# Cross attention with a mixture-of-experts stage: bias columns, norm seeds, tanh and first units' splits at other ticks, mask rows at once

## Chip, cores, metric

One Trainium2 chip, one core. The metric is the device time of the whole kernel in microseconds. Three runs of the kernel before gave 1059.28, 1064.75 and 1064.88 us, median 1064.75.

## What is computed

Eight batches of 512 tokens, 256 wide, with a context of 512 tokens, 512 wide, all in float32:

```python
x = x + xattn(ctx, layernorm(x), mask, mask, W_src, b_src, W_tgt, b_tgt, W_out, b_out)
x = x + ffn(layernorm(x), ...)
# xattn: k, v = split((ctx @ W_src.T + b_src) * mask); q = (x @ W_tgt.T + b_tgt) * mask
#        8 heads of 32; softmax(q k / sqrt(32)) with masked keys at -inf; times v
#        cat(x, update) @ W_out.T + b_out
# ffn:   scores = sigmoid(l2norm(x) @ l2norm(gate).T), top 8 of 16 experts, weights / their sum
#        sum over experts of w * (silu(x @ wg) * (x @ wu)) @ wd, and a shared expert beside them
```

## The kernel before, in words

Every engine runs the same ordered list of steps, and each takes from it what concerns it, in order. Between engines there are only semaphore waits; an instruction that waits holds up all that is behind it on its engine. A matrix product in near-float32 precision is made of three: each operand is split into a high part (a rounding copy, mostly on ScalarE) and a low part (a subtraction on VectorE or GpSimd), and TensorE does hi*hi, hi*lo and lo*hi.

**The attention stage.** `attention()` gives each step a tick, a number on a common scale, and sorts the steps by tick (equal ticks in the order in which they were listed). Work is in 16 groups (g), two per batch, of four heads each. A group takes 16 ticks: each tick holds one matmul for the row maxima (`max`, L732, in PSUM banks 0 and 1, reduced by VectorE at L1201 14 ticks ahead of the group) and one scores matmul (`scores`, L748), whose result goes through the exponential on ScalarE (L868, the helper of all ScalarE copies) into one of seven `e_buf` slots. GpSimd adds four of these (`e_add`, L1407) for the softmax sums, and `attend` multiplies them with v (L759) and ones (L772). The projections of later groups, q, k, v and y, lie between at ticks of their own, in three PSUM banks used in turn. `hi_q`, `hi_k`, `lo_k` split q and k, and `stack` copies the splits by DMA from the SP queue (ScalarE's queue has a part of the first two) into `q_stack` and `k_stack`; row 96 of `k_stack` is the mask bias (`bias_row`), row 97 of `q_stack` the negated maxima (`shift`, `neg`). The high part of the next group's q may be written only when the stacks of the group before have landed.

**The start.** The first steps stand in a list `first` at tick -42.4. The bias of v goes through the output weights: VectorE spreads it to 128 columns (L1182, the tile shares space with `e_buf`), TensorE multiplies (L790), VectorE adds to the bias rows (L1185), and GpSimd adds these to x (`x_bo`). All of that is the step `bo` at tick -13.8, behind the operations of the second batch's layer norm (`ln1`, ticks from -26.2).

**The mask.** For each batch c the mask row comes broadcast to 128 partitions; `mask_bias` on VectorE (L1155) turns one row of 512 elements into 0 or -1e30, at 2.7 ticks after the beginning of each pair of groups, in one of two row buffers.

**The way into the second stage.** For batch 0, `ln2` (33 steps on VectorE, GpSimd and ScalarE; steps 8 and 9 compute `ve` on GpSimd, L1359 and L1361, steps 10 and 11 are VectorE's seeds for the inverse root, L1070 and L1072, then GpSimd goes on) lies in group 13; `gating` (16 steps on VectorE, of which the third multiplies the logits by the norm, L1267, and the fourth needs ScalarE's tanh) in group 14. Six units of experts (`gate_up` 0 to 5) are laid in group 15 and behind it. For a unit, TensorE computes gate and up into two banks; ScalarE the silu (for the first four units as a tanh), VectorE the products (L1301, L1304, L1309), ScalarE the high part hh, VectorE the low part; `down` multiplies by the third weight matrix. All of ScalarE's and VectorE's part of a unit stands at the tick of its `gate_up`. `early_w` splits weights on ScalarE and GpSimd; `turn_c` turns the combine weights, and `load_c` spreads them by DMA over 128 partitions.

**The second stage.** The other 130 units follow in a fixed order, each `gate_up` with the `down` of two units before.

## Time and profile before

| | us |
|---|---|
| median of three runs | 1064.75 |
| lowest, highest | 1059.28, 1064.88 |
| span of the profiled execution | 1056.2 |
| TensorE busy | 1012.5 (96%) |
| VectorE busy | 647.5 (61%) |
| ScalarE busy | 465.9 (44%) |
| GpSimd busy | 389.0 (37%) |

The span is that of the first to the last instruction of one execution; no other time is given for it. Shares are averages over the whole span: GpSimd, VectorE and ScalarE do most of their work in the first 480 us. A matmul counts as busy until its modelled end, at either clock.

### The profile page before, as it was taken

The numbers are of one execution on the slowest core, as the hardware profiler recorded it, in microseconds if no ns is written. First come the engines' busy times: TensorE is split into PE (matmuls) and PEld (weight loads), VectorE is DVE, ScalarE is ACT, GpSimd is POOL, SyncE is SP. The second block draws the span as 40 slices with busy tenths as digits, with TensorE's granted clock in tenths as the row PEclk, the third lists the DMA queues.
The fourth block names the chain that finished last, engine by engine and source line by source line (L and its number), as shares of the span: only waits on it lengthen the run. The fifth ranks groups of instructions, "written<-read, shape, count | busy, mean of one in ns | idle before, by whom it ended". The sixth has DMA issues, their size and how long they took to land.

```text
span 1056.2 us, 14941 instructions
## 1 busy us (share of the span) xinstructions
PE 1012.5 (96%) x5198; PEld 773.3 (73%) x5198; DVE 647.5 (61%) x1469; ACT 465.9 (44%) x865; POOL 389.0 (37%) x355
## 2 busy tenths in 40 slices
PE   4789999999999998899999999999999999999998
PEld 3656767676767665567888888888888888888886
DVE  5877777877777557355565555555555555555544
ACT  3346565656665646545323323333333333332322
POOL 3379797879797967345210010010010100100000
PEclk9899999999999999999999999999999999999999
DMA  7343433434333223324222121121220230221220
GB/s 239 104 131 78 131 81 111 108 84 131 73 110 75 65 65 105 92 86 131 75 80 61 52 80 50 61 81 40 72 80 31 71 90 20 91 80 31 93 68 20
DMA packets 65674, 87.87 MB, mean 83 GB/s; under 512 B 10720, under 2 KB 31088, under 8 KB 65600
## 3 DMA queue, kind: packets, MB, share of 16 engines
q1 hardware_dynamic: 63680, 84.83, 28.0%
q10 hardware_dynamic: 1920, 2.10, 0.6%
q8 instruction: 41, 0.67, 0.3%
q14 instruction: 33, 0.27, 0.1%
HBM read 56.97 MB, written 4.46 MB: 58 GB/s over the span
## 4 chain that ended last, share of the span: by engine, by line
PE 91%; DVE 4%; ACT 2%; SPq 1%; issue 1%; DMA 1%; POOL 0%; DVEq 0%; ACTq 0%
PE ps L653 50%; PE pst L653 18%; PE ps L732 6%; PE ps L759 5%; PE pst L748 5%; PE ps L659 4%; PE ps L772 1%; DVE mx L1201 1%; ACT e_buf L868 1%; SPq L606 1%; PE ps L811 1%; SPq L541 1%; ACT ctx_h L868 0%; DVE wsrc_l L1148 0%; PE ps L812 0%
## 5 line engine op out<-in xcount | busy, mean ns | idle before, releaser
L653 PE MATMUL ps<-x_h,weights 128*128 128x512 f32 x1088 | 365.6, 397 | 1.4 <-DVE x L1194 0.8
L653 PEld LDWEIGHTS ps<-x_h,weights 128*128 128x128 f32 x1088 | 204.5, 188 | 51.8 <-issue 1.0
L1201 DVE TENSOR_REDUCE mx<-ps 128x1 f32<-128x512 f32 x256 | 173.3, 685 | 81.8 <-PE ps L732 80.9
L868 ACT ACTIVATE hh<-qb 128x512 fp32r<-128x512 f32 x136 | 86.0, 632 | 296.4 <-DVE qb L1315 273.7
L653 PE MATMUL ps<-x_l,weights 128*128 128x512 f32 x544 | 214.6, 395 | 0.0
L653 PE MATMUL pst<-hh,weights 128*128 128x512 f32 x544 | 194.6, 399 | 0.0
L1304 DVE TENSOR_TENSOR qb<-ps,sg 128x512 f32<-128x512 f32 x136 | 94.1, 692 | 160.2 <-PE ps L653 153.8
L868 ACT ACTIVATE e_buf<-pst 128x512 f32<-128x512 f32 x256 | 147.4, 596 | 92.8 <-PE pst L748 81.8
L1317 DVE TENSOR_TENSOR hl<-qb,hh 128x512 fp32r<-128x512 f32 x136 | 94.3, 693 | 95.0 <-ACT hh L868 95.0
L1407 POOL TENSOR_TENSOR e_sums<-e_sums,e_buf 128x1024 f32<-128x1024 f32 x60 | 143.5, 2391 | 7.2 <-ACT e_buf L868 1.2
L1359 POOL TENSOR_SCALAR ve<-mv 128x4 f32<-128x4 f32 x8 | 1.8, 226 | 347.1 <-DVE mv L1242 347.1
L653 PEld LDWEIGHTS ps<-x_l,weights 128*128 128x128 f32 x544 | 102.1, 188 | 24.6
L748 PE MATMUL pst<-q_stack,k_stack 98*128 98x512 f32 x256 | 108.4, 425 | 12.1 <-ACT e_buf L868 12.0
L868 ACT ACTIVATE sg<-ps 128x512 f32<-128x512 f32 x136 | 81.1, 596 | 86.6 <-PE ps L653 86.6
L653 PEld LDWEIGHTS pst<-hh,weights 128*128 128x128 f32 x544 | 102.2, 188 | 23.3 <-DVE hl L1317 0.8
L732 PE MATMUL ps<-k_stack,q_stack 97*128 97x512 f32 x256 | 109.7, 430 | 6.7 <-DVE mx L1201 6.2
L653 PE MATMUL pst<-hl,weights 128*128 128x512 f32 x272 | 107.3, 394 | 0.0
L1315 DVE TENSOR_TENSOR qb<-qb,cb 128x512 f32<-128x512 f32 x124 | 87.4, 705 | 4.2
L1407 POOL TENSOR_TENSOR e_sums<-e_buf 128x1024 f32<-128x1024 f32 x30 | 71.8, 2394 | 48.8 <-PE ps L772 48.3
L732 PEld LDWEIGHTS ps<-k_stack,q_stack 97*128 97x128 f32 x256 | 49.2, 193 | 46.0 <-issue 29.1
L748 PEld LDWEIGHTS pst<-q_stack,k_stack 98*128 98x128 f32 x256 | 49.4, 194 | 27.1 <-ACT e_buf L868 16.6
L759 PE MATMUL ps<-e_buf,v_buf 128*32 128x512 f32 x512 | 62.1, 603 | 0.0
(159 smaller groups left out, 1391.5 us busy)
## 6 DMA issues: line engine op xcount, KB each, us to landing
cb<-combine_scratch SPq DMA_DIRECT2D x128, 256.0 KB, 3.2
q_stack<-q_h SPq DMA_DIRECT2D x128, 64.0 KB, 2.0
k_stack<-k_h SPq DMA_DIRECT2D x124, 64.0 KB, 2.0
ctx_raw<-in_ctxT SPq DMA_DIRECT2D x7, 1024.0 KB, 5.2
q_stack<-q_l SPq DMA_DIRECT2D x64, 64.0 KB, 2.0
out_x<-ob SPq DMA_DIRECT2D x16, 256.0 KB, 2.2
k_stack<-k_l SPq DMA_DIRECT2D x62, 64.0 KB, 2.0
x<-in_x SPq DMA_DIRECT2D x7, 512.0 KB, 6.5
```

The source lines that it names most:

```text
L541: e.dma_start(f32(KS[g % 2][at:at + 32, h, :]), f32(src[32 * h:32 * h + 32, :])).then_inc(sem(f"stack{g % 2}{h}"), 16)
L653: ins = engine.matmul(dst, lhsT, rhs, start=start and n == 0, stop=stop and n == len(terms) - 1)
L659: ins = engine.transpose(dst, src, ID[0:k, 0:k])
L732: engine.matmul(ps, QS[z][0:97, h, 128 * q:128 * q + 128], KS[z][0:97, h, :], start=True, stop=True).then_inc(sem("s_max"), 1)
L748: engine.matmul(YP[:, m % 2, :], KS[z][0:98, h, 128 * k:128 * k + 128], QS[z][0:98, h, :], start=True, stop=True).then_inc(sem("s_t"), 1)
L759: ins = engine.matmul(OP[32 * i:32 * i + 32, :], VB[:, b % 2, k, hh + i, :], EB[:, SLOTS[8 * g + 4 * (i // 2) + k], i % 2, :], start=k == ...
L868: return engine.activation(dst, src, func, **kw)
L1201: engine.tensor_reduce(MX[:, g % 2, h // 2, h % 2, q:q + 1], bank(step), AX.X, ALU.max).then_inc(sem("max"), 1)
L1304: engine.tensor_tensor(QB[:, w, :], GP[n][1], SG[:, w, :], ALU.mult).then_inc(sem("hq"), 1)
L1315: engine.tensor_tensor(QB[:, w, :], QB[:, w, :], CB[:, m % NC, :], ALU.mult).then_inc(sem("hc"), 1)
L1317: engine.tensor_tensor(HLB[:, n % NH, :], QB[:, w, :], f32(HHB[:, n % NH, :]), ALU.subtract).then_inc(sem("h_lo"), 1)
L1407: engine.tensor_tensor(ES[:, a, :, :], first, EB[:, SLOTS[n + 1 + i], :, :], ALU.add).then_inc(sem("e_add"), 1)
```

## The change

The steps that change place or kind:

- `mask_bias`: one step in `first`. A new DMA on SP, ahead of the small bias loads, brings all eight mask rows into partitions 32 to 39 of `shift_rows`, and one VectorE operation of 8 x 512 converts them. `bias_row` reads the row of its batch. The seven later operations, and the waits for them on SP and GpSimd, go; `shift_rows` is half as long per partition.
- `bo`: VectorE's two column copies become the step `bv`, in `first` ahead of v; the TensorE part `bo` follows v and `out_q` there; the addition `bo_add` stays at -13.8. q of the second group moves ahead of both halves of v.
- the splits and first stack of the third group (p = 2): 2.6 ticks later.
- `ln2` of batch 0: the first ten steps from 2.6 in steps of 0.3 (before 3.1 in steps of 0.4), the others from 8 in steps of 0.33 (before they began at 7.1).
- `gating` of batch 0: three steps as before, the others from 6.8 in steps of 0.35 (before from 5.5 in steps of 0.4); the tanh goes with the fourth (6.8) and no more with the first (4.3). `turn_c` and four `load_c` from 12.7 to 14.8.
- the units: `silu`, `unit`, `hi_h`, `lo_h` are steps of their own; for the first six they are 0.5, 0.6, 2.4 and 2.5 ticks behind their `gate_up`. In the second stage they directly follow it, in the same order as before.

```diff
-        if half == 0:
-            at(t + 2.7, ("mask_bias", c))
-        at(t + 5.4, ("hi_q", p))
-        at(t + 6.4, ("hi_k", p))
-        at(t + 7.1, ("lo_k", p))
-        at(t + 7.1, ("stack", p, 0))
+        late = 2.6 if p == 2 else 0
+        at(t + 5.4 + late, ("hi_q", p))
+        at(t + 6.4 + late, ("hi_k", p))
+        at(t + 7.1 + late, ("lo_k", p))
+        at(t + 7.1 + late, ("stack", p, 0))
...
-             ("load_ctx", 1), ("k", 0, 0), ("k", 0, 1), ("mask_bias", 0), ("ws_hi", 1), ...
+             ("load_ctx", 1), ("k", 0, 0), ("k", 0, 1), ("mask_bias",), ("ws_hi", 1), ...
-             ("v", 0, 0, 0), ("q", 1), ("v", 0, 0, 1), ("out_q", 1), ("out_v", 0, 0), ("bias_row", 1)]
+             ("q", 1), ("bv",), ("v", 0, 0, 0), ("v", 0, 0, 1), ("out_q", 1), ("bo",), ("out_v", 0, 0), ("bias_row", 1)]
...
-    at(-13.8, ("bo",))
+    at(-13.8, ("bo_add",))
...
-        at(t + 3.1 + 0.4 * i, s)
+        at(t + (2.6 + 0.3 * i if i < 10 else 8 + 0.33 * (i - 10)), s)
...
-        at(t + 4.3 + 0.4 * i, s)
-    at(t + 12.7, ("turn_c", 0), *[("load_c", m) for m in range(NC)])
+        at(t + (4.3 + 0.4 * i if i < N_TANH else 6.8 + 0.35 * (i - N_TANH)), s)
+    at(t + 14.8, ("turn_c", 0), *[("load_c", m) for m in range(NC)])
...
+    for n, when in enumerate((3.6, 7.2, 13, 16.2, 25.3, 26.6)):
+        at(t + when + 0.5, ("silu", n))
+        at(t + when + 0.6, ("unit", n))
+        at(t + when + 2.4, ("hi_h", n))
+        at(t + when + 2.5, ("lo_h", n))
...
-        shift_rows = s1("shift_rows", [97, 2, S], F32R)
-        MR, NM, OR = shift_rows[96:97, :, :], shift_rows[0:8, 0, 0:128], shift_rows[64:65, 0, :]
+        shift_rows = s1("shift_rows", [65, S], F32R)
+        MR, NM, OR = shift_rows[32:32 + B, :], shift_rows[0:8, 0:128], shift_rows[64:65, :]
...
+                    engine.dma_start(f32(MR), mask).then_inc(sem("ld_rows"), 16)
...
-                    dve.wait_ge(*mask_loaded(b))
-                    if b > 1:
-                        dve.wait_ge(*row_loaded(2 * b - 3))
-                    engine.tensor_scalar(MR[:, b % 2, :], MB[96:97, b % 2, :], 0.0, MASKED, ALU.is_equal,
-                                         ALU.mult).then_inc(sem("mask_bias"), 1)
+                    dve.wait_ge(sem("ld_rows"), 16)
+                    engine.tensor_scalar(MR[:, :], f32(MR[:, :]), 0.0, MASKED, ALU.is_equal, ALU.mult).then_inc(
+                        sem("mask_bias"), 1)
```

## Rows read from the trace of the kernel before

**Rows 1.** The page's picture in 40 slices: TensorE's busy tenths.

```profile
PE   4789999999999998899999999999999999999998
```

**Rows 2.** The list of waits on TensorE: total us, times, longest us.

```profile
PE pst L748 <- ACT e_buf L868: 12.0, 12, 2.5
```

**Rows 3.** Table by stretches; after the engines' busy us: granted clock, DMA share, GB/s.

```profile
core 0: us, PE busy (x) PEld busy (x) DVE busy (x) ACT busy (x) POOL busy (x), PEclk, DMA share, GB/s
31.40:35.30 3.90, 3.87 (x15) 3.51 (x16) 2.05 (x9) 0.00 (x0) 1.57 (x1) 0.56 0.42 103
35.30:44.90 9.60, 9.05 (x55) 7.53 (x54) 7.50 (x20) 3.88 (x8) 3.74 (x3) 1.00 0.36 112
48.70:56.10 7.40, 7.05 (x19) 4.52 (x17) 4.84 (x11) 4.53 (x10) 5.25 (x5) 0.54 0.44 106
390.00:395.00 5.00, 5.00 (x30) 2.48 (x29) 2.23 (x4) 1.37 (x3) 3.36 (x6) 0.66 0.35 85
415.00:420.00 5.00, 5.00 (x28) 2.88 (x27) 4.97 (x20) 4.00 (x9) 4.95 (x4) 0.75 0.26 79
```

**Rows 4.** Timeline of the start, SP and TensorE: start us, us, what, idle before.

```profile
2.71 0.88 SPq L533 DMA_DIRECT2D mask_rows<-in_mask  x1
...
21.81 0.39 PE L653 MATMUL ps<-wsrc_h,ctx_h 128*128 128x256 f32 x1 [1.21 <-DVE wsrc_l L1148]
...
31.43 1.68 PE L790 MATMUL ps<-e_buf 128*128 128x256 f32 x4 [3.44 <-DVE e_buf L1182]
```

**Rows 5.** Timeline of the start, VectorE.

```profile
21.68 0.74 DVE L1175 SCALAR_TENSOR_TENSOR k_l<-ps,bk,k_h 128x512 fp32r<-128x512 f32 x1
24.93 0.75 DVE L1170 SCALAR_TENSOR_TENSOR f_buf<-ps,bt,mask_rows 128x512 f32<-128x512 f32 x1 [2.51 <-PE ps L653]
...
30.86 0.47 DVE L1182 TENSOR_SCALAR e_buf<-ones_sb,bv 128x128 f32<-128x128 f32 x2
33.15 0.42 DVE L1185 TENSOR_TENSOR bo_rows<-ps,bo_rows 128x256 f32<-128x256 f32 x1 [1.82 <-PE ps L790]
```

**Rows 6.** Timeline 55 to 60 us, GpSimd, VectorE, TensorE.

```profile
55.80 2.38 POOL L1407 TENSOR_TENSOR e_sums<-e_buf 128x1024 f32<-128x1024 f32 x1
...
56.30 2.17 DVE L1155 TENSOR_SCALAR shift_rows<-mask_rows 1x512 fp32r<-1x512 f32 x1
...
59.25 0.50 PE L732 MATMUL ps<-k_stack,q_stack 97*128 97x512 f32 x1 [0.97 <-DVE mx L1201]
```

**Rows 7.** All mask operations: duration ns min/median/max, first and last start us.

```profile
L1155 DVE TENSOR_SCALAR shift_rows<-mask_rows x8: 424/1556/2171, 18.6 to 353.3; 1x512 fp32r<-1x512 f32 x8
```

**Rows 8.** Timeline 62 to 64 us, ScalarE and TensorE.

```profile
62.77 0.63 ACT L868 ACTIVATE q_h<-f_buf 128x512 fp32r<-128x512 f32 x1 [5.23 <-DMA k_stack<-k_l]
...
63.93 0.50 PE L748 MATMUL pst<-q_stack,k_stack 98*128 98x512 f32 x1 [1.35 <-ACT e_buf L868]
```

**Rows 9.** Timeline 388 to 390 us, VectorE and TensorE.

```profile
388.17 0.17 DVE L1070 TENSOR_SCALAR rs_a<-ve 128x8 int32<-128x8 int32 x1 [2.82 <-POOL ve L1361]
...
389.29 0.47 PE L732 MATMUL ps<-k_stack,q_stack 97*128 97x512 f32 x1 [2.29 <-DVE mx L1201]
```

**Rows 10.** Timeline 410 to 414 us, GpSimd, VectorE, TensorE.

```profile
410.55 2.35 POOL L1407 TENSOR_TENSOR e_sums<-e_sums,e_buf 128x1024 f32<-128x1024 f32 x1
...
411.18 1.80 DVE L1267 TENSOR_TENSOR lg<-lg,rn 128x64 f32<-128x64 f32 x1
...
413.90 0.59 PE L748 MATMUL pst<-q_stack,k_stack 98*128 98x512 f32 x1 [2.46 <-ACT e_buf L868]
```

**Rows 11.** Timeline 434 to 452 us, ScalarE and TensorE.

```profile
434.19 0.60 ACT L868 ACTIVATE sum_sb<-ps 128x512 f32<-128x512 f32 x1
...
441.38 0.63 ACT L868 ACTIVATE hh<-qb 128x512 fp32r<-128x512 f32 x1 [2.82 <-DVE qb L1309]
...
442.55 0.98 PE L748 MATMUL pst<-q_stack,k_stack 98*128 98x512 f32 x2 [2.47 <-ACT e_buf L868]
...
451.45 0.47 PE L653 MATMUL ps<-x_h,weights 128*128 128x512 f32 x1 [0.64 <-DVE sg L1301]
```

**Rows 12.** The page's costliest groups, one product of a unit on VectorE.

```profile
L1304 DVE TENSOR_TENSOR qb<-ps,sg 128x512 f32<-128x512 f32 x136 | 94.1, 692 | 160.2 <-PE ps L653 153.8
```

More of the change, by code:

```diff
@@ L47 @@
 N_LN1, N_LN2, N_GROWS, N_GATE = N_SMALL1 + 4, N_SMALL2 + 4, 3 + rsqrt_steps(1) + 3, 16
+N_TANH = 3
 TODO = [(b, e) for b in range(B) for e in range(E + 1)]
@@ L121, in attention @@
              ("ctx", 0, 3), ("ws_hi", 0), ("q", 0), ("ws_lo", 0), ("out_q", 0), ("hi_q", 0),
-             ("load_ctx", 1), ("k", 0, 0), ("k", 0, 1), ("mask_bias", 0), ("ws_hi", 1), ("hi_k", 0), ("ws_lo", 1), ("lo_k", 0),
+             ("load_ctx", 1), ("k", 0, 0), ("k", 0, 1), ("mask_bias",), ("ws_hi", 1), ("hi_k", 0), ("ws_lo", 1), ("lo_k", 0),
              ("bias_row", 0), ("stack", 0, 0), ("stack", 0, 1), ("stack", 0, 2), ("stack", 0, 3), ("wo",),
-             ("v", 0, 0, 0), ("q", 1), ("v", 0, 0, 1), ("out_q", 1), ("out_v", 0, 0), ("bias_row", 1)]
+             ("q", 1), ("bv",), ("v", 0, 0, 0), ("v", 0, 0, 1), ("out_q", 1), ("bo",), ("out_v", 0, 0), ("bias_row", 1)]
     at(-42.4, *first)
@@ L259, in order @@
             load_c(b * E + min(e, E) + NC)
-            out.append(("gate_up", n))
+            out += [("gate_up", n), ("silu", n), ("unit", n), ("hi_h", n), ("lo_h", n)]
             if b + 1 < B:
@@ L583, in sync_program @@
                     sp.wait_ge(sem("q_f"), 2 * b - 2)
-                    sp.wait_ge(sem("mask_bias"), b - 1)
                     load_mask(engine, b)
@@ L591, in sync_program @@
                     g = step[1]
-                    sp.wait_ge(sem("mask_bias"), g // 2 + 1)
+                    sp.wait_ge(sem("mask_bias"), 1)
                     if g > 1:
                         sp.wait_ge(*scores_done(g - 2, 3))
-                    row = MR[:, (g // 2) % 2, :].rearrange("a (h s) -> a h s", h=1).to_broadcast([1, 4, S])
+                    row = MR[g // 2:g // 2 + 1, :].rearrange("a (h s) -> a h s", h=1).to_broadcast([1, 4, S])
                     engine.dma_start(f32(KS[g % 2][96:97, :, :]), f32(row)).then_inc(sem(f"bias_row{g % 2}"), 16)
@@ L616, in sync_program @@
                     sp.wait_ge(sem("x_bo"), B)
-                    sp.wait_ge(sem("mask_bias"), B)
                     for e in range(NR):
@@ L1020, in scalar_program @@
                     copy(X2h[:, b % 2, j, :], bank(step)).then_inc(sem("x2_hi"), 1)
-                elif kind == "gating" and step[2] == 0:
+                elif kind == "gating" and step[2] == N_TANH:
                     b = step[1]
@@ L1035, in scalar_program @@
                     act.wait_ge(sem("ut_lo"), NG)
-                elif kind == "gate_up":
+                elif kind == "silu":
                     n = step[1]
@@ L1048, in scalar_program @@
                         copy(SG[:, n % 2, :], GP[n][0], ACT.Silu).then_inc(sem("silu"), 1)
+                elif kind == "hi_h":
+                    n = step[1]
                     b, e = TODO[n]
@@ L1150, in vector_program @@
                 elif kind == "mask_bias":
-                    b = step[1]
-                    dve.wait_ge(*mask_loaded(b))
-                    if b > 1:
-                        dve.wait_ge(*row_loaded(2 * b - 3))
-                    engine.tensor_scalar(MR[:, b % 2, :], MB[96:97, b % 2, :], 0.0, MASKED, ALU.is_equal,
-                                         ALU.mult).then_inc(sem("mask_bias"), 1)
+                    dve.wait_ge(sem("ld_rows"), 16)
+                    engine.tensor_scalar(MR[:, :], f32(MR[:, :]), 0.0, MASKED, ALU.is_equal, ALU.mult).then_inc(
+                        sem("mask_bias"), 1)
                 elif kind == "lo_x":
@@ L1177, in vector_program @@
                                                     sem("k_lo"), 1)
-                elif kind == "bo":
+                elif kind == "bv":
                     for k in range(2):
@@ L1183, in vector_program @@
                             sem("bv_cols"), 1)
+                elif kind == "bo_add":
                     dve.wait_ge(sem("bo_t"), 1)
-                    engine.tensor_tensor(BO[:, :], bank(step)[:, 0:D], BO[:, :], ALU.add).then_inc(sem("bo"), 1)
+                    engine.tensor_tensor(BO[:, :], bank(("bo",))[:, 0:D], BO[:, :], ALU.add).then_inc(sem("bo"), 1)
                 elif kind == "out_y":
@@ L1291, in vector_program @@
                     dve.wait_ge(sem("y"), COUNT["y", B - 1, 1, 1])
-                elif kind == "gate_up":
+                elif kind == "unit":
                     n = step[1]
@@ L1315, in vector_program @@
                         engine.tensor_tensor(QB[:, w, :], QB[:, w, :], CB[:, m % NC, :], ALU.mult).then_inc(sem("hc"), 1)
+                elif kind == "lo_h":
+                    n = step[1]
+                    w = n % 2
                     dve.wait_ge(sem("h_hi"), n + 1)
@@ L1422, in gpsimd_program @@
                     pool.wait_ge(sem("y_add"), COUNT["out_y", B - 1, 0, 1])
-                    pool.wait_ge(sem("mask_bias"), B)
                 elif kind in ("early_w", "split_w"):
```

## The prediction, made before the result was known

> **What bounds the kernel now.** I read the picture in slices first: TensorE is busy nine tenths or more in every slice from the fourth on but two, and from about 475 us to the end it has no gap worth a row [rows 1]. So the second half is TensorE's own work, which the edits leave alone, and a gain must come from the holes before 475 us. Second, the list of waits: the largest item is the scores matmul waiting for an exponential on ScalarE (12.0 us in 12 places) [rows 2]. Third, the table by stretches, for the clock: behind three of the holes, and once more near 50 us, the granted clock is a mix of 1.2 and 2.4 GHz [rows 3]. A clock of 0.56 over 3.9 us loses 0.44 x 3.9 = 1.7 us of work; 0.54 over 7.4 us loses 3.4; 0.66 over 5 us loses 1.7; 0.75 over 5 us loses 1.25. Last, the timelines around each hole, to see which instruction was in front of the one TensorE needed.
>
> The sum is made against the profiled span, 1056.2 us. The three runs lie 3.1 to 8.7 us above it (median 1064.75), and the page has no other time of that execution, so the difference found here is taken off the median.
>
> **Start, 20 to 45 us.** Before, TensorE waits 1.21 us for the second half of the source weights, and later 3.44 us for the two bias-column copies [rows 4], which stand on VectorE behind 34 small norm operations although their input landed long ago; the copies take 0.47 us [rows 5]. After it, the clock is low for 1.7 us worth of work [rows 3]. The change puts q of the second group into the first hole (six matmuls fill it) and the copies ahead of the norm chain. TensorE alone would gain 1.21 + 3.44 + 1.7 = 6.35 us. VectorE allows less: its f_buf operation starts at 24.93 after 2.51 us of waiting [rows 5]; with q early it follows k_l (21.68 + 0.74) and the copies (0.47) [rows 5], at about 22.9, so 2.0 us earlier. It then no longer runs the copies in the chain (0.47) nor waits for the bo matmul (1.82) [rows 5], and of its 2.1 us of idle time in 35.3 to 44.9 [rows 3] I count half, 1.0. That is 5.3 us. What ends last is then the row maxima on VectorE, no more the hole. I take the smaller bound, **-5.3**; the ends are -3.4 (the hole alone) and -6.4.
>
> The new load of the mask rows is one more issue on SP ahead of the bias loads, at most 0.88 us, what the larger mask load took there [rows 4]; its followers are the bias loads and ones rows, first wanted at 17.8 us or later. The eight-row operation replaces a one-row one of 0.42 us (the minimum of the eight) [rows 7]; as elements per partition stay 512, I take the same. Both 0, at worst +0.9.
>
> **Mask operation of the second batch and the third group's splits, 55 to 65 us.** At 56.30 the mask operation takes 2.17 us, as long as GpSimd's e_sums is still running; TensorE then waits 0.97 us for the next maximum [rows 6]. It goes. ScalarE stands 5.23 us before q_h of the third group, since the last k_stack transfer of the second has not landed; exponentials are queued behind and TensorE waits 1.35 us [rows 8]. With 2.6 ticks more, two or three scores' exponentials come first. The landing itself stays where it is relative to k_l, so some 0.4 us of waiting may stay in ScalarE, beside TensorE's long matmuls. **-2.3**; ends 0 and -3.2 (with the smaller gaps around). The SP queue meets the third group's stack 2.6 ticks later, about ten ticks before its first maximum: no cost.
>
> The six other mask operations take 0.5 to 1.6 us each [rows 7], but TensorE has no wait for a maximum behind any of them: 0, at best -0.5. The waits removed from SP, GpSimd and the mask loads are passed long before in the trace: 0.
>
> **Norm seeds, 380 to 392 us.** The seed on VectorE waits 2.82 us for ve from GpSimd, which stands behind an e_sums; maxima are queued behind the seed, and TensorE waits 2.29 us [rows 9]. The change does two things: the statistics and so ve come 1.3 ticks earlier, ahead of q_l and that e_sums, and the seeds 0.9 tick later. ve is then computed a whole e_sums (2.4 us, as in rows 6) and a q_l earlier than the 388 of now, and the seed has its turn not before the matmuls that now run out at 387 (389.29 - 2.29). Behind it goes the low clock, 1.7 us [rows 3]. VectorE and ScalarE have room there. q_l comes 0.6 us later by the two ve operations, and what GpSimd does behind it, so 0.4 us is given back: 2.29 + 1.7 - 0.4 = **-3.6**. Ends 0 and -4.5.
>
> **Tanh, 410 to 420 us.** TensorE waits 2.46 us for an exponential behind the tanh on ScalarE, which waits for lg times rn on VectorE (1.80 us, to 412.98) [rows 10]. With the tanh 2.5 ticks later the exponentials run on. But VectorE's 1.80 us is not moved. Two more maxima can be written ahead, then TensorE waits for VectorE: the next maximum can start only at about 413.2, one reciprocal behind 412.98, and frees its bank at 413.9, which is where the hole ends now. Counting the two matmuls that run ahead, the hole shrinks from 2.46 to about 1.2, and VectorE, busy 4.97 of the 5 us from 415 on [rows 3], sets the pace, so the low clock behind it (1.25) [rows 3] is worth little. **-1.3**; ends 0 and -3.7. turn_c comes 2.1 ticks later, and the combine weights with it; their first use, in unit 0, is behind two waits of its own and comes later too: 0, at worst +1.
>
> Which resource that is: the two slow VectorE rows, 2.17 and 1.80 us, end where a GpSimd e_sums ends (55.80 + 2.38, 410.55 + 2.35) [rows 6, 10]. The Trainium skill, "SBUF — State Buffer", section "Who interferes with whom", says that the port pair of the two engines is held for a whole instruction and the other blocks; by that rule, the trace agrees, and the last two gating operations, moved from 0.9 to 0.2 ticks before an e_sums issue, could be caught by it. It is a rival below.
>
> **First units, 428 to 456 us.** hh of unit 1 on ScalarE waits to 441.38 with three exponentials behind it, and TensorE waits 2.47 us [rows 11]. The split takes hh behind them. But half a tick puts the silu behind others as well, and I follow the queue: silu of unit 0 (tick 244.1) is now behind out_o (243.8), whose sums arrive at 434.19 [rows 11]: out_o 2 x 0.5, so the silu is at 435.2. VectorE's three operations at 0.7 [rows 12] end at 437.9; hh 0, spread and the weight split (0.6, 0.6, 0.9) come next, and only then the exponential of 246.5, at 440.0. But the exponentials of the next scores are no more behind hh of unit 1. The hole of 2.47 us breaks into pieces of 0.3 to 0.9, and the attention matmuls start 1.0 us earlier. Then unit 2: its silu has the tick 253.5, the same as the last score, which was listed first. Now VectorE's sg of this unit starts as soon as both halves of gate_up are there, and TensorE waits 0.64 us for it [rows 11]. Afterwards the silu comes behind that score (0.4) and its exponential (0.5), and takes 0.6 itself: sg and gate_up 3 are 1.4 to 1.5 us later, a loss of 1.4. Net +0.4, less 0.2 for a short wait near 470 us that goes with the earlier ut_h: **+0.2**. Ends -2.5 (all of the hole) and +2.
>
> Sum: -5.3 - 2.3 - 3.6 - 1.3 + 0.2 = **-12.3 us**: span 1044, median 1064.75 - 12.3 = **1052.4 us**. With the ends that are likely together, 1048 to 1057.
>
> **Rivals.**
> A. *The clock near 50 us stays high too.* The hole ahead of the low stretch, a wait for the maxima behind the split of k, remains, which speaks against; for it speaks that the larger hole of 3.44 us before it goes, and that the hole of 1.35 us at 62.6 [rows 8] had no low clock behind it. It gives back 3.4 us more [rows 3]: 1049.0.
> B. *VectorE is caught by the shared port.* lg times rn and the last gating operations each wait for an e_sums, up to 2.35 us [rows 10]; one more such wait in 410 to 422 cancels the tanh's gain and 1.1 more: 1052.4 + 2.4 = 1054.8. For it: both engines are nearly full there.
> C. *The next engine takes the gains.* Only the head holds (5.3), since GpSimd and VectorE don't move up with TensorE: 1059.4. Against: their waits there are mostly for TensorE.
> D. *The clock falls in the start* (slower). With VectorE setting the pace from 27 to 45 us, TensorE has many small gaps, and the low level could hold on. A microsecond at the low level costs half; from 25 us more of it than now the change loses, and from 27 to 66 us at the low level, 39 less the 10.2 now low (twice 1.7 + 3.4), costs 14.4, so 1052.4 + 14.4 = 1066.8. Against: 35.3 to 44.9 us had 6% of gaps and the full clock [rows 3].
>
> The Trainium skill, "TensorE: Matmul & The Clock Gate", section "HAM oscillation — how this bites in real kernels", says that idle time of TensorE brings the low clock; the trace agrees at 28, 387 and 411 us and disagrees at 440, where 2.47 us of idleness had none. By the rule alone A would be less likely, as a hole stays in front.
>
> **Numbers.** Forecast 0.58, A 0.14, B 0.13, C 0.11, D 0.04. About 0.5%, 5.3 us, is what a measurement here tells from no change. Faster by more (below 1059.4): the forecast, A, B and part of C, 0.86; within 0.5%: 0.10; slower 0.04. The runs of before lie 5.6 us apart, and the median after may fall in either part, so the range reaches from A less 5 to beyond C: 1043.5 to 1060.5.
>
> **What would show it.** Right: no matmul at L790 with a wait of microseconds, and the first maximum of batch 0's second score row over 3 us earlier; q_h of the third group with less than 1 us of waiting; the seed without a wait for ve and no maximum wait near 385; after the tanh a wait for mx of about 1 us in place of one for e_buf; gate_up 3 waiting for sg about 2 us. Wrong: L1201 waits of several microseconds in the start, a clock below 1 in new places, or holes that come back as L748 waits before 475 us. If the distance from 475 us to the end changed by more than 1 us, the argument of the first paragraph falls.

## The result, and the profile after

| | before | after |
|---|---|---|
| median of 20 runs, us | 1064.49 (1058.21 to 1067.37) | 1058.83 (1054.72 to 1061.16) |
| ratio, 95% interval | | 0.9949 [0.9934, 0.9963] |
| profiled execution: time, span, granted clock | span 1056.2, clock 0.992 | 1055.66, 1053.5, 0.992 |

The kernel became 5.4 us faster (0.51% of 1064.5), where 12.3 was forecast. By the experiments the start gave 6.4 us, as much as forecast for it and a little more; the 7 us forecast for the other parts were not there. In the runs after, the device time lies 2.1 to 2.2 us above the span.

The table by stretches around the holes, first of the profile before (columns as in [rows 3]: stretch, length, busy us and instructions of each engine, granted clock, DMA share, GB/s), then of the one after.

```profile
26.00:31.00 5.00, 1.99 (x16) 1.67 (x14) 4.83 (x37) 1.54 (x2) 2.35 (x1) 1.00 0.55 132
45.00:53.00 8.00, 6.11 (x18) 3.99 (x18) 7.06 (x13) 5.07 (x11) 2.73 (x3) 0.74 0.34 82
390.00:402.00 12.00, 11.42 (x66) 7.54 (x64) 6.55 (x11) 5.63 (x12) 9.63 (x16) 0.86 0.24 57
409.00:416.00 7.00, 4.54 (x22) 3.40 (x22) 5.66 (x16) 3.79 (x9) 6.86 (x5) 0.86 0.41 123
```

After, the same stretches:

```profile
26.00:31.00 5.00, 4.17 (x30) 3.69 (x28) 4.82 (x36) 2.14 (x3) 2.72 (x2) 1.00 0.64 152
45.00:53.00 8.00, 7.14 (x22) 4.78 (x21) 5.55 (x16) 5.59 (x11) 6.45 (x5) 0.70 0.42 101
390.00:402.00 12.00, 9.82 (x47) 6.08 (x49) 5.78 (x9) 8.05 (x16) 7.24 (x12) 0.72 0.44 114
409.00:416.00 7.00, 5.47 (x23) 2.77 (x27) 5.37 (x24) 4.92 (x11) 7.00 (x6) 0.76 0.20 60
```

The first line is the start: TensorE's 1.99 us of work in 26 to 31 became 4.17, because the hole of [rows 4] is gone. The other lines show what was not forecast: near 48, 395 and 412 us the granted clock is lower than before.

The holes on TensorE after the change (timeline: start us, duration, what, idle time before it and what ended it):

```profile
31.01 0.50 PE L737 MATMUL ps<-k_stack,q_stack 97*128 97x512 f32 x1 [0.84 <-DVE mx L1206]
...
71.88 0.47 PE L737 MATMUL ps<-k_stack,q_stack 97*128 97x512 f32 x1 [3.27 <-issue]
...
385.09 0.27 PE L664 MATMUL ps<-ident_sb,mx 128*8 128x128 f32 x1 [0.72 <-DVE mx L1206]
...
394.40 0.63 PE L753 MATMUL pst<-q_stack,k_stack 98*128 98x512 f32 x1 [1.20 <-ACT e_buf L873]
396.36 0.79 PE L753 MATMUL pst<-q_stack,k_stack 98*128 98x512 f32 x1 [0.90 <-ACT e_buf L873]
...
409.77 0.50 PE L737 MATMUL ps<-k_stack,q_stack 97*128 97x512 f32 x1 [1.66 <-DVE mx L1206]
411.54 0.69 PE L737 MATMUL ps<-k_stack,q_stack 97*128 97x512 f32 x1 [0.66 <-DVE mx L1206]
...
419.50 0.47 PE L737 MATMUL ps<-k_stack,q_stack 97*128 97x512 f32 x1 [0.84 <-DVE mx L1206]
...
434.12 0.47 PE L753 MATMUL pst<-q_stack,k_stack 98*128 98x512 f32 x1 [0.90 <-ACT e_buf L873]
...
449.57 0.47 PE L658 MATMUL ps<-x_h,weights 128*128 128x512 f32 x1 [2.04 <-DVE sg L1306]
```

Read beside [rows 4, 6, 8 to 11]: each hole named there went, and each but those of the start has a successor. The 0.97 and 1.35 us near 60 became 3.27 at 71.88; the 2.29 at 389 became 0.72, 1.20 and 0.90; the 2.46 at 414 became 1.66, 0.66 and 0.84; the 2.47 at 442.6 and 0.64 at 451 became 0.90, 0.58 (438.28) and 2.04. [<-issue] in the line of 71.88 says only that the profile shows nothing that was waited for; the first experiment shows what it was.

How far ahead of the kernel before each point is, in us of the two profiles (attends counted from 0, two to a group):

| start of | before | after | ahead |
|---|---|---|---|
| first matmul | 11.22 | 12.02 | -0.80 |
| attend 0 | 67.56 | 59.68 | 7.88 |
| attend 1 | 77.70 | 73.11 | 4.59 |
| attend 25 | 376.13 | 371.60 | 4.53 |
| attend 26 | 392.44 | 385.29 | 7.15 |
| attend 27 | 405.06 | 400.71 | 4.35 |
| attend 29 | 431.34 | 429.07 | 2.27 |
| last gate_up matmul that waits | 474.65 | 472.27 | 2.38 |

7.9 us were gained by 60 us, and 3.3 of them lost in one hole. The steady stretch carried the 4.5. The seeds' hole gave 2.6, and by attend 27 it was given back, 2.1 more by attend 29.

**Hole at 71.88.** The SP queue after (issues: start us, duration):

```profile
41.06 0.53 SPq L612 DMA_DIRECT2D q_stack<-q_h  x1
...
55.59 0.59 SPq L547 DMA_DIRECT2D k_stack<-k_l  x1
...
60.52 0.51 SPq L612 DMA_DIRECT2D q_stack<-q_h  x1
...
68.61 0.59 SPq L547 DMA_DIRECT2D k_stack<-k_l  x1
69.25 0.63 SPq L602 DMA_DIRECT2D k_stack<-shift_rows  x1
```

The second group's stacks take SP from 41.06 to 56.2, 24 issues of about 0.6 us. Before, they began at 45.77. Their last landing frees q_h of the third group, at 57.68 after, with 0.46 us of waiting where [rows 8] had 5.23. The third group's stacks follow, two of them ahead of its bias row, which is issued only at 69.25, and the first maximum's matmul of that group, at 71.88, needs the row.

**Holes at 394 to 396 and 409 to 411.**

```profile
381.96 1.81 DVE L1077 TENSOR_SCALAR rs_a<-ve 128x8 int32<-128x8 int32 x1
...
393.01 0.22 POOL L1387 TENSOR_SCALAR rn<-v 128x4 f32<-128x4 f32 x1
...
393.27 0.60 ACT L873 ACTIVATE xm<-x,nmr,rs 128x256 f32<-128x256 f32 x1 [0.95 <-POOL rn L1387]
...
406.55 2.37 POOL L1415 TENSOR_TENSOR e_sums<-e_sums,e_buf 128x1024 f32<-128x1024 f32 x1
...
407.15 1.85 DVE L1272 TENSOR_TENSOR lg<-lg,rn 128x64 f32<-128x64 f32 x1
...
410.50 0.39 DVE L1275 TENSOR_SCALAR sc<-sc 128x64 f32<-128x64 f32 x1 [0.78 <-ACT sc L873]
```

The seed no longer waits for ve (2.82 us in [rows 9]), but it takes 1.81 us in place of 0.17, beside an e_sums; and xm on ScalarE now comes before rn and waits for it, with exponentials behind. Counted from attend 25, rn starts 21.4 us later (before: 21.9), but the first xm 21.7 us later (before: 24.3): the norm's work on GpSimd came hardly sooner, its user on ScalarE much. lg times rn stands through an e_sums as in [rows 10], and TensorE now waits for the maxima behind it.

### The profile page after: what moved, and what is told of

It is laid out like the page before. It is cut to its first block, busy times and chain, and to the rows that moved or that the text cites. A ratio compares the mean times of both kernels' runs of the same rounds, so it can differ in the third digit from the quotient of the medians.

```text
span 1053.5 us, 14928 instructions
## 1 busy us (share of the span) xinstructions
PE 1011.3 (96%) x5198; PEld 772.9 (73%) x5198; DVE 638.3 (61%) x1462; ACT 467.2 (44%) x865; POOL 389.7 (37%) x355
## 3 DMA queue, kind: packets, MB, share of 16 engines
q1 hardware_dynamic: 63696, 84.85, 27.9%
## 4 chain that ended last, share of the span: by engine, by line
PE 91%; DVE 4%; ACT 2%; issue 1%; POOL 1%; DMA 0%; ACTq 0%; DVEq 0%; POOLq 0%
PE ps L658 50%; PE pst L658 18%; PE ps L737 6%; PE ps L764 6%; PE pst L753 5%; PE ps L664 4%; PE ps L777 1%; DVE mx L1206 1%; PE ps L816 1%; ACT e_buf L873 1%; ACT ctx_h L873 0%; DVE wsrc_l L1155 0%; PE ps L817 0%; DVE xn L1131 0%; PE ps L771 0%
```

## The experiments

Each was timed in five rounds beside the kernel before on the same chip; ratios are to that kernel. Most have five or six runs, the tenth twelve, so that an interval is mostly 0.002 wide to either side, 2.4 us. "Changed kernel" is the one after.

**First: bias row of the third group ahead of the second stack.**

```diff
-        at(t + 13.4, ("bias_row", p))
+        at(t + (13.05 if p == 2 else 13.4), ("bias_row", p))
```

> The changed kernel, with the bias row of the third group issued on SP ahead of that group's second stack (tick 13.05 for p = 2 instead of 13.4). Theory 1: the 3.27 us hole of TensorE at 68.6 to 71.9 us in the changed kernel is the wait for this one transfer, which SP issues at 69.25, behind six others of 0.6 us each. Then the hole shrinks by about 3 us and the second attend burst (73.1 us) comes at about 70. Rival: the hole is the wait for the third group's first stack or for the k split itself; then it stays at 3 us. In the median of many runs theory 1 expects about 3 us less than the changed kernel, 1056 against 1059.

Ratio 0.9930 [0.9909, 0.9950], median 1056.67. The hole at 71.88 is gone and attend 1 begins at 70.36. The next fence (ScalarE, TensorE) shows where it went:

```profile
80.21 0.63 ACT L873 ACTIVATE q_h<-f_buf 128x512 fp32r<-128x512 f32 x1 [5.43 <-DMA k_stack<-k_l]
...
81.38 0.50 PE L753 MATMUL pst<-q_stack,k_stack 98*128 98x512 f32 x1 [3.18 <-ACT e_buf L873]
```

The cause of the hole is shown, and so is that mending it only moves it on: q_h of the fourth group waits for the third group's landings, as the third's waited before. Attend 2 begins at 88.13 (after: 85.94), and the ratio's interval overlaps that of the changed kernel.

**Second: third group's splits at their old ticks.**

```diff
-        late = 2.6 if p == 2 else 0
+        late = 0
```

> The changed kernel, with the third group's splits back at their old ticks (late = 0). Theory 1: SP's chain of issues from k_l of the second group to the bias row of the third is what ends last, and the later ticks cost it at most 0.8 us; so the hole before 71.9 shrinks by less than 1 us, a hole of about 1 us comes back near 59 us behind q_h waiting for k_stack, and the second attend burst stays within 1 us of 73.1. Rival 2: the 2.6 ticks themselves (4 us) delay the chain; then the burst comes 2 to 3 us earlier and the kernel is faster by that.

Ratio 0.9940 [0.9917, 0.9964], 1057.43. A hole of 2.88 us for an exponential at 59.84 stands in place of the 3.27; attend 1 is at 73.63 (after: 73.11), the first matmul 0.24 later. The late splits bring nothing that can be measured. Nor does taking away the mask operation alone: with it and the old splits (seventh, below) that place has two holes, 1.04 and 1.08 us, and here, without it, one of 2.88.

**Third: only start, mask rows and the third group's splits kept.** Norm, gating, tanh, turn_c and unit steps at the ticks of before.

```diff
-N_TANH = 3
+N_TANH = 0
...
-        at(t + (2.6 + 0.3 * i if i < 10 else 8 + 0.33 * (i - 10)), s)
+        at(t + 3.1 + 0.4 * i, s)
...
-        at(t + (4.3 + 0.4 * i if i < N_TANH else 6.8 + 0.35 * (i - N_TANH)), s)
-    at(t + 14.8, ("turn_c", 0), *[("load_c", m) for m in range(NC)])
+        at(t + 4.3 + 0.4 * i, s)
+    at(t + 12.7, ("turn_c", 0), *[("load_c", m) for m in range(NC)])
...
-        at(t + when + 0.5, ("silu", n))
-        at(t + when + 0.6, ("unit", n))
-        at(t + when + 2.4, ("hi_h", n))
-        at(t + when + 2.5, ("lo_h", n))
+        at(t + when, ("silu", n), ("unit", n), ("hi_h", n), ("lo_h", n))
```

> The changed kernel with norm seeds, gating, tanh, turn_c and first units back at the ticks of the kernel before: only start, mask rows and third group's splits are changed. Theory: the head gives 4.6 us (the attend bursts from the second on lie 4.6 us earlier) and the tail parts together give nothing or cost 2 us, so this kernel is as fast as the changed one or up to 2 us faster: ratio to before 0.993 to 0.996. Rival: the tail parts carry half or more of the gain in the median of many runs (through the low clock behind the holes of 2.3 to 2.5 us, which falls in some runs only), then this one is slower than the changed kernel by 2 us or more: 0.997 to 0.999.

Ratio 0.9940 [0.9917, 0.9964], 1057.14: as much as the whole change. The old holes (2.29, 2.49, 2.48 us) are back and cost nothing against the new ones.

**Fourth: silu and unit at gate_up's tick.**

```diff
-        at(t + when + 0.5, ("silu", n))
-        at(t + when + 0.6, ("unit", n))
+        at(t + when, ("silu", n), ("unit", n))
```

> The changed kernel with silu and products of the first six units back at the tick of their gate_up, and only the splits hi_h and lo_h 2.4 ticks later. Theory: the 2.04 us hole before gate_up 3 is the silu of unit 2 standing behind the last exponential; it goes back to 0.6, and the hole of 0.9 at 434 us shrinks, while the 2.5 us hole behind hh of unit 1 stays away: from the attend burst of 429.07 to gate_up 6 (43.2 us in the changed kernel, 43.3 before) about 41 us. Rival: the holes return as waits for sg and exponentials elsewhere, total unchanged within 0.5 us.

Ratio 0.9911 [0.9889, 0.9933], 1054.50. From attend 29 to the last gate_up matmul that waits (469.05) it is 40.37 us (after: 43.20; before: 43.31), with two holes over 0.4 us in between, 0.41 us for an exponential and 0.64 us for sg. So the split of hh is a gain, and the half tick took it back. The distance is 40.3 to 40.4 us in all six profiles with this form of the units.

**Fifth: gating, tanh and turn_c back, in the fourth's kernel.**

```diff
-N_TANH = 3
+N_TANH = 0
...
-        at(t + (4.3 + 0.4 * i if i < N_TANH else 6.8 + 0.35 * (i - N_TANH)), s)
-    at(t + 14.8, ("turn_c", 0), ...
+        at(t + 4.3 + 0.4 * i, s)
+    at(t + 12.7, ("turn_c", 0), ...
```

> The kernel of the fourth experiment (silu and unit at gate_up's tick, split of hh later), and in it the tanh, the gating operations and turn_c at the ticks that they had before the change. Theory 1: the tanh's move brought nothing, because the 1.85 us that lg times rn takes on VectorE stayed where it is and the maxima wait for it; it turned one hole of 2.46 us into three of 1.66, 0.66 and 0.84 us (3.16 together). Then the holes go back to one of about 2.5 us for an exponential and the time is 0 to 1.5 us lower than the fourth experiment's: ratio 0.990 to 0.991. Rival, the prediction's: the move is worth 1.3 us, and the time is that much higher: ratio 0.9923. What the clock does behind the hole may add or take 1.7 us in a single profile.

Ratio 0.9913 [0.9891, 0.9936], 1054.62: nothing. One hole of 2.49 us stands in place of the fourth's 1.67, 0.66 and 0.86.

**Sixth: xm 1.4 ticks later, in the fourth's kernel.**

```diff
-        at(t + (2.6 + 0.3 * i if i < 10 else 8 + 0.33 * (i - 10)), s)
+        at(t + (2.6 + 0.3 * i if i < 10 else 8 + 0.33 * (i - 10) + (1.4 if i >= N_SMALL2 else 0)), s)
```

> The fourth experiment's kernel with the four xm operations of the second norm 1.4 ticks later and its seeds as after the change. Theory 1: the seeds' move works, but the tighter chain that follows it (0.33 ticks a step) puts xm on ScalarE 0.95 us ahead of rn on GpSimd, with exponentials queued behind; these are the holes of 1.20 and 0.90 us near 395 us and, with the low clock of 6.8 us behind them, the greater part of what the seeds failed to give. Then both holes and the low clock near 395 go, and the time falls by 2.1 us and up to 3.4 more: ratio 0.986 to 0.989. Rival: x_h and with it the logits then come later, the hole moves to 400 to 410 us, and the ratio stays at 0.991.

Ratio 0.9912 [0.9889, 0.9934], 1053.95: the rival. The waits for exponentials went, and the transpose of xm itself waits:

```profile
397.76 1.06 PE L663 MATMUL ps<-ident_sb,xm 128*128 128x128 f32 x4 [1.80 <-ACT xm L872]
```

**Seventh: the start alone, on the kernel before.**

```diff
-             ("v", 0, 0, 0), ("q", 1), ("v", 0, 0, 1), ("out_q", 1), ("out_v", 0, 0), ("bias_row", 1)]
+             ("q", 1), ("bv",), ("v", 0, 0, 0), ("v", 0, 0, 1), ("out_q", 1), ("bo",), ("out_v", 0, 0), ("bias_row", 1)]
...
-    at(-13.8, ("bo",))
+    at(-13.8, ("bo_add",))
```

> The kernel before with the start alone changed: q of the second group ahead of v, bias columns ahead of the norm chain, the bo sum as a step of its own; mask operations, third group's splits, norm seeds, tanh and units are those before. Theory 1: in the head one chain sets the pace, SP's issues of the second group's stacks, which begin when k_l of that group is there; the start brings k_l about 4.7 us forward, and nothing else in the head counts. Then the stacks of the second group are issued from about 41 us, the mask operation at 52 to 56 us and the wait before q_h of the third group cost nothing in the end, attention group 1 begins within 1 us of where it begins after the change (73.1 us), and the ratio is 0.9945 to 0.997, the whole of the change's gain. Rival, the prediction's: the mask operation and the stall at the third group's splits (2.3 us) are on the path, and this kernel gains 2 us less than the change: ratio 0.9965 to 0.998.

Ratio 0.9940 [0.9916, 0.9963], median 1057.78 against 1064.02: 6.4 us. SP, VectorE, ScalarE and TensorE in its head:

```profile
40.34 0.53 SPq L606 DMA_DIRECT2D q_stack<-q_h  x1
...
51.07 2.25 DVE L1155 TENSOR_SCALAR shift_rows<-mask_rows 1x512 fp32r<-1x512 f32 x1
...
54.09 0.50 PE L732 MATMUL ps<-k_stack,q_stack 97*128 97x512 f32 x1 [1.04 <-DVE mx L1202]
...
57.33 0.63 ACT L868 ACTIVATE q_h<-f_buf 128x512 fp32r<-128x512 f32 x1 [5.02 <-DMA k_stack<-k_l]
...
58.49 0.50 PE L748 MATMUL pst<-q_stack,k_stack 98*128 98x512 f32 x1 [1.08 <-ACT e_buf L868]
```

The mask operation of 2.25 us, the stall before q_h (5.02) and both holes of [rows 6, 8] are still there, and attend 1 begins at 72.50, ahead even of the changed kernel's 73.11. Counted from the first matmul it is at 61.52 (before 66.48, after 61.09). The two holes were real and their removal was not worth anything. The ratio is a little below the range expected (0.9945 to 0.997), within its interval.

**Eighth: bias rows of two groups early, the fourth group's splits late, in the fourth's kernel** (and y of that group 1.1 to 2.2 ticks later, to free its bank).

```diff
-        late = 2.6 if p == 2 else 0
+        late = 2.6 if p in (2, 3) else 0
...
-        at(t + 13.4, ("bias_row", p))
+        at(t + (13.05 if p in (2, 3) else 13.4), ("bias_row", p))
```

> The fourth experiment's kernel with the bias rows of the third and fourth groups ahead of the second stack on SP, the fourth group's splits 2.6 ticks later like the third's, and y of that group later by 1 to 2 ticks so that its bank comes free. In the first experiment the hole of 3.27 us before the first maximum of the third group went and came back at 81 us, where ScalarE stood 5.43 us before q_h of the fourth group with exponentials behind it. Theory 1: the two are one chain (SP's issues, 0.6 us each, 24 for a group), and each wait in front of it only has to be kept away from the exponentials. Then neither hole is there, attention group 2 begins at 82.5 to 83.5 us in place of 85.6, and the ratio is 0.988 to 0.989. Rival: SP is the bound itself, so the hole comes back once more, before the fourth group's first maximum (about 83 to 90 us) or later, and the ratio stays at 0.991.

Ratio 0.9921 [0.9899, 0.9943], 1055.90: the rival's time, but not its reason. A hole came back a third time, now for k_l (ScalarE, VectorE, TensorE):

```profile
78.93 0.62 ACT L873 ACTIVATE q_h<-f_buf 128x512 fp32r<-128x512 f32 x1
...
80.92 0.67 ACT L873 ACTIVATE k_h<-ps,bk 128x512 fp32r<-128x512 f32 x1
...
81.63 0.75 DVE L1179 SCALAR_TENSOR_TENSOR k_l<-ps,bk,k_h 128x512 fp32r<-128x512 f32 x1 [1.44 <-ACT k_h L873]
...
82.43 0.39 PE L658 MATMUL ps<-wout_h,xt_h 128*128 128x256 f32 x1 [2.69 <-DVE k_l L1179]
```

q_h of the fourth group no longer stands idle for a landing. The hole is the price of the late splits themselves: k_l is the last reader of k's PSUM bank (`bank_free`), k_h before it now stands behind xn on ScalarE, and TensorE needs the bank. SP's queue as the bound is not shown by it.

**Ninth: start, mask rows and the fourth's form of the units; all else as before.** The lines of the third experiment but for the units', the second's, and:

```diff
-        at(t + when + 0.5, ("silu", n))
-        at(t + when + 0.6, ("unit", n))
+        at(t + when, ("silu", n), ("unit", n))
...
-        late = 2.6 if p == 2 else 0
+        late = 0
```

> The changed kernel with the third group's splits, the second norm, the gating and tanh, and turn_c at the ticks of before; kept are the start, the mask rows at once, and the units in the fourth experiment's form (silu and unit at gate_up's tick, split of hh 2.4 ticks later). Theory 1: the start alone is worth 0.994 (seventh experiment) and this form of the units takes the hole of 2.47 us before an exponential, with its low clock, and nothing of gate_up 3; the other moves are worth nothing. Then the ratio is 0.991, that of the fourth, fifth and sixth experiments. Rival, the prediction's: the seeds' and the third group's moves are worth 3.6 and 2.3 us, and this kernel is 3 to 6 us slower than the fourth: ratio 0.994 to 0.997.

Ratio 0.9890 [0.9868, 0.9913], median 1052.07: the fastest kernel of this study, 11.7 us under before by the ratio. The moves that it leaves out (third group's splits, seeds and norm, gating, tanh, turn_c) were forecast at 7.2 us, together with the mask rows, which it keeps, and are worth none; it lies 2.4 us under the fourth by medians taken on two chips, with intervals that overlap. No run took the mask rows out of it.

**Tenth: the changed kernel without its start.**

```diff
-             ("q", 1), ("bv",), ("v", 0, 0, 0), ("v", 0, 0, 1), ("out_q", 1), ("bo",), ("out_v", 0, 0), ("bias_row", 1)]
+             ("v", 0, 0, 0), ("q", 1), ("v", 0, 0, 1), ("out_q", 1), ("out_v", 0, 0), ("bias_row", 1)]
...
-    at(-13.8, ("bo_add",))
+    at(-13.8, ("bv",), ("bo",), ("bo_add",))
```

> The changed kernel with its start undone: v ahead of q of the second group, the bias columns and the bo sum behind the norm chain where they stood before; all other steps of the change stay. Theory 1: the start is the whole gain, and mask rows, third group's splits, seeds, tanh and units together are worth nothing: ratio 0.998 to 1.001. Rival, the prediction's: they are worth 2.3 + 3.6 + 1.3 - 0.2 = 7.0 us: ratio 0.9935. In the profile the hole of about 3.4 us before the bo matmuls is back near 31 us, and the second group's stacks are issued from about 46 us in place of 41.

Ratio 1.0005 [0.9988, 1.0022], median 1064.34. All other parts together are worth nothing. TensorE and SP show the hole back, and the stacks 5.6 us later than after:

```profile
32.32 1.55 PE L795 MATMUL ps<-e_buf 128*128 128x256 f32 x4 [3.42 <-DVE e_buf L1186]
...
46.65 0.53 SPq L612 DMA_DIRECT2D q_stack<-q_h  x1
```

**Eleventh: lg times rn behind the e_sums, tanh later, in the fourth's kernel.**

```diff
-        at(t + (4.3 + 0.4 * i if i < N_TANH else 6.8 + 0.35 * (i - N_TANH)), s)
+        at(t + (4.3 + 0.4 * i if i < 2 else 6.9 if i < N_TANH else 8.2 + 0.35 * (i - N_TANH)), s)
```

> The fourth experiment's kernel with lg times rn 1.8 ticks later, behind the GpSimd e_sums that it now stands through (1.85 us for what is elsewhere 0.2), and the tanh and what follows 1.4 ticks later with it. Theory 1: the operation is long only because the shared port is held; at the new tick it meets a GpSimd operation of 1.3 us or less, or none, takes 0.2 to 1.3 us, and the holes before the maxima (1.66 + 0.66 + 0.84 us) shrink to under 1.6 together, with less low clock behind: 1 to 3 us less than the fourth experiment, ratio 0.988 to 0.990. Rival: VectorE has no room there at all (its maxima come at the pace of TensorE), so the later gating operations make the same holes: ratio 0.991 to 0.992.

Ratio 0.9905 [0.9882, 0.9927], 1053.81. The place is as theory 1 has it: the operation takes 0.84 us, and the holes shrink from the fourth's 3.19 to 1.15 us (0.50 and 0.65). But another gating operation is caught in turn, and the gain in time is within the interval:

```profile
412.25 0.84 DVE L1271 TENSOR_TENSOR lg<-lg,rn 128x64 f32<-128x64 f32 x1
...
420.15 2.72 DVE L1287 TENSOR_TENSOR sc<-sc,rep 128x64 f32<-128x64 f32 x1
```

**Twelfth: the ninth's kernel with the units as the change has them.**

```diff
-        at(t + when, ("silu", n), ("unit", n))
+        at(t + when + 0.5, ("silu", n))
+        at(t + when + 0.6, ("unit", n))
```

> The ninth experiment's kernel with the units as the change has them: silu and unit 0.5 and 0.6 ticks behind gate_up. Theory 1, the prediction's step: half a tick puts silu behind other work, which takes back what the split of hh gives, so these ticks are worth +0.2 us against the units of before, and 3 to 4 us less than the ninth experiment's: ratio 0.9925 to 0.994, with the wait of gate_up 3 for sg at 2.0 us. Rival: in the changed kernel the late silu costs only together with the late turn_c and gating, which are not here: ratio 0.989 to 0.990, and gate_up 3 waits 0.6 us.

Ratio 0.9931 [0.9915, 0.9947], 1057.09: theory 1. gate_up of unit 3 waits 2.04 us for sg, and the half tick costs 4.4 us against the ninth (0.0041 x 1064). The profiles agree: from attend 29 to the last gate_up matmul that waits it is 44.71 us, in the ninth 40.37.

## Why the prediction was half right

Of 12.3 us, 5.3 were forecast for the start and came; 7.0 were forecast for the other parts and did not. What failed in the three of them that were to gain is the same step: a hole was taken off the sum, and nothing or too little was put in for what TensorE would wait for next.

**Start, -5.3: right, and its reason too.** It gave 6.4 (0.006 x 1064, interval 3.9 to 8.9). f_buf, counted at 2.0 us sooner, starts 11.52 us behind the first matmul (23.54; before 13.71), 2.2 sooner, with k_l and the copies in front, and the bo addition no longer waits. The bound that was named, VectorE's maxima, shows after as the wait of 0.84 us at 31.01. The low clock behind the hole went (31 to 35 us: 0.60 before, 1.00 after), but in 35 to 45 us it fell from 0.99 to 0.90, which nobody had counted. How the gain carries through the head fits the SP queue: the second group's stacks begin 4.7 us sooner (41.06 against 45.77), and the wait for their landings moves with them. That is argued from the traces; no run changed SP's work alone.

**Mask operation and third group's splits, -2.3: wrong (experiments 2, 7, 10).** The step that failed is the sentence "The SP queue meets the third group's stack 2.6 ticks later, about ten ticks before its first maximum: no cost." I counted the stack and not the bias row, which on SP stands behind two stacks, 8.7 us from 60.52 to 69.20; the row is what the first maximum lacked. Behind it is a larger fault: I took the two holes off the sum without asking what the same point in time would wait for next. By the first experiment the mended hole returns one group later, since the fourth group's splits wait for the landings of the third; by the eighth, splits laid late enough to avoid that wait hold their PSUM bank too long; and with the old splits and no mask operation it is 2.88 us (second) and 2.92 (ninth), at 58 to 60 us. That SP's issues alone are the bound is not shown; no run took issues off that queue.

**Norm seeds, -3.6: wrong.** The mechanism named was there: no wait for ve, a hole of 0.72 us in place of 2.29, and attend 26 at 2.6 us more ahead. "VectorE and ScalarE have room there" is what failed: room was not the question, for ScalarE waits there for GpSimd, which the sum left out. The steps behind the seeds were made denser (0.33 for 0.4 ticks), and xm met rn too early; two holes followed, and the clock of 390 to 402 us is 0.72 (0.86 before), 1.7 us more lost. Putting xm later (sixth) gave nothing, as its transpose then waits 1.80 us for it. No run moved the seeds alone; that they are worth nothing follows from the ninth against the fourth, with the second and the fifth. Attend 25 to 27 takes 27.9 to 29.1 us in the nine profiles with the new ticks and 28.8 to 30.5 in the five with the old.

**Tanh, -1.3: mechanism right, size wrong.** "Then TensorE waits for VectorE" came true: 1.66 us as against 1.2. The term that was mis-sized is the hole that stays: the sum put it at 1.2 us once, and behind it come 0.66 us, after a gating operation that waits 0.78 us for the tanh (410.50), and 0.84, 3.16 in all for 2.46. Fifth: 0.

**First units, +0.2: right in its steps, and in size as far as can be told.** The queue was followed correctly: the pieces are 0.90 and 0.58 us, gate_up 3 waits 2.04 us, 1.4 more than before. The twelfth lies 1 us under the seventh by their ratios, within both intervals. But 43.31 us, from attend 29 to the last waiting gate_up, was a low value for the old form: its other two profiles (third, seventh) have 46.2 and 46.1, as low clock follows the hole of 2.47 us there. That term was put at nothing. The undelayed form, at 40.4, gains 3 us on the one and 5.7 on the others; the ninth, which has it, lies 5.3 us under the seventh. Ninth against twelfth shows the price of the half tick, 4.4 us.

**Six other mask operations and removed waits: 0, right.** VectorE's busy time falls by 8.6 us in 90 to 350 us (195.8 to 187.2), and TensorE's stays within 0.1 us. **New load, 0, at worst +0.9: open.** TensorE's first matmul is at 11.87 to 12.26 us in eight of the twelve profiles with the load, at 11.0 to 11.2 in three and at 9.87 in one; without it at 10.98 and 11.22. Two profiles are too few to tell.

**Rivals.** C came nearest, only the start holds (1059.4 against 1058.83), and I gave it 0.11. Its reason (GpSimd and VectorE don't move up) is not what happened; what each next matmul needed, on SP, ScalarE and GpSimd, did it; the number was met by luck. B happened as a mechanism, at the seed (1.81 us) and at `lg<-sc,ts`, and was not decisive. A and D did not.

Two counts in the reading were off by one and carry nothing: 35 small norm operations stand ahead of the copies, not 34, and the picture has three slices below nine tenths from the fourth on, the last one included, not two.

**The clock.** I priced low stretches from one profile. The next lines are of 350 to 430 and 430 to 476 us, the first two of the kernel before, the last two of the seventh experiment, which has the same code and the same holes there (2.23, 0.53, 2.44 and 2.47 us against 2.29, 0.53, 2.46 and 2.47):

```profile
350.00:430.00 80.00, 74.11 (x439) 50.73 (x440) 49.62 (x98) 45.85 (x92) 61.57 (x50) 0.96 0.31 83
430.00:476.00 46.00, 41.41 (x235) 26.28 (x234) 20.26 (x38) 23.43 (x46) 17.39 (x31) 1.00 0.28 80
```

```profile
350.00:430.00 80.00, 74.18 (x430) 51.87 (x430) 48.38 (x95) 44.08 (x87) 58.63 (x48) 0.91 0.29 79
430.00:476.00 46.00, 41.42 (x216) 25.63 (x209) 18.89 (x37) 22.23 (x42) 15.40 (x29) 0.93 0.25 78
```

Close behind the hole of 2.47 us, first in the kernel before, then in the seventh experiment:

```profile
442.50:449.30 6.80, 6.75 (x44) 3.16 (x45) 0.84 (x2) 3.25 (x7) 1.28 (x1) 1.00 0.15 39
```

```profile
439.70:446.50 6.80, 6.80 (x34) 1.87 (x34) 0.78 (x2) 2.03 (x4) 1.27 (x1) 0.54 0.15 38
```

From attend 24 to the last gate_up matmul that waits the one needs 110.9 us, the other 115.8. The clock takes 0.05 x 80 + 0.07 x 46 = 7.2 us more in the second, part of it in idle stretches where it costs nothing. So the same hole sometimes has 1.2 GHz behind it and sometimes not, and the profile before was a lucky one: its clock is 0.992, the mean of 50 other runs of that kernel 0.986, 14.8 us lost in place of 8.4 (span times one less clock). The changed kernel's 20 runs lose 11.6. By this count 3 of its 5.4 us come by way of the clock; the rest of the span, times the clock, went from 1046.9 to 1044.6. It is an estimate: it takes low clock in idle stretches for a loss, and the runs of before that have a clock on record are those beside the experiments, on four chips.

The Trainium skill, "TensorE: Matmul & The Clock Gate", section "HAM oscillation — how this bites in real kernels", has idleness bring the low clock. The runs agree that low stretches follow holes (0.54 above), and add that one profile cannot say behind which (1.00 above).

## What to carry to other kernels

A hole in TensorE's timeline is worth what remains when everything else due at that time is checked, on every queue: take it away, then ask for each input of the next few matmuls when it comes, counting each DMA issue at its measured 0.6 us and those queued ahead of it. Moving a step by half a tick means a place in another order on every engine; it cost 4.4 us here, so place it by the order that results and try the unmoved form beside it. Before adding up several local gains, run them one at a time: here two edits (the start and the split of hh, undelayed) gave 11.7 us, the half tick took 4.4 back, and the others gave nothing.

## What the hardware showed that was not expected

The first microseconds differ between executions of the same start. VectorE's four xn and GpSimd's ctx_l, first in the profile after, then in that of the fourth experiment, which has the same code there:

```profile
8.41 3.46 DVE L1131 TENSOR_SCALAR xn<-x,mv,rs 128x256 f32<-128x256 f32 x4
...
8.44 1.26 POOL L1356 TENSOR_TENSOR ctx_l<-ctx_raw,ctx_h 128x512 fp32r<-128x512 f32 x1 [7.01 <-ACT ctx_h L873]
```

```profile
8.34 1.38 DVE L1130 TENSOR_SCALAR xn<-x,mv,rs 128x256 f32<-128x256 f32 x4
...
9.48 3.20 POOL L1355 TENSOR_TENSOR ctx_l<-ctx_raw,ctx_h 128x512 fp32r<-128x512 f32 x2 [8.06 <-ACT ctx_h L872]
```

In the first, where GpSimd begins a microsecond earlier, the four take 3.46 us in place of 1.38, and the first matmul is at 12.02 in place of 9.87. Over the fourteen profiles the four take one of three times: 1.38 us (once), 2.33 (five times) or 3.29 to 3.46 (eight times), about a microsecond apart; GpSimd's operation takes 1.3. A point in the head must therefore be counted from the first matmul. The longest single small operation was `sc<-sc,rep` in the eleventh experiment, 2.72 us for an operation of 64 elements a partition that took 0.20 in the profile after; it began beside one GpSimd operation (419.15, 1.29 us) and ended at 422.87, when the e_sums of 420.39 (2.40 us) had ended.

Over the 20 runs after, span and granted clock go together (correlation -0.93): 1052.6 to 1059.1 us at 0.993 to 0.987. 0.006 x 1055 = 6.3 us is nearly the whole spread of 6.5.
